# A fused attention and mixture-of-experts block: five shared-expert tiles moved into the start, their gates on GpSimd, and the small transposes behind the weighing

## The reference, cut to what matters

```
def _L0_attn_ref(x, Wq, Wk, Wv, norm_w, Wo, bo, diff_weight):
    ...
    scores = jnp.einsum('bqhif,bkhif->ibhqk', qs, ks_) * scale
    atts = jax.nn.softmax(scores, axis=-1)
    att = atts[0] - diff_weight * atts[1]
    o = jnp.einsum('bhqk,bkhe->bqhe', att, vs)
    rms = jax.lax.rsqrt(jnp.mean(o * o, axis=(-2, -1), keepdims=True) + eps)
    normed = (o * rms * norm_w).reshape(b, s, e)
    return (normed @ Wo.T + bo) * (1.0 - diff_weight)

def _L0_ffn_ref(x, Wg, Ws1, Ws3, Ws2, We1, We3, We2):
    gates = jax.nn.sigmoid(xf @ Wg)
    vals, idx = jax.lax.top_k(gates, TOP_K)
    ...
    shared = jax.nn.silu(xf @ Ws1) * (xf @ Ws3) @ Ws2
    h = jax.nn.silu(jnp.einsum('td,edf->tef', xf, We1)) * jnp.einsum('td,edf->tef', xf, We3)
    routed = jnp.einsum('tef,efd,te->td', h, We2, w)
    out = (shared + routed) / (N_SHARED + TOPK)
    ...
x = x + attention(xn) + ffn(xn)
```

## Time and profile before

| | |
|---|---|
| median of 3 runs | 604.8 us (603.62 to 604.98) |
| profiled execution | 604.48 us, of which the span from first to last instruction is 602.5 us |
| PE busy | 95% of the span |
| DVE busy | 78% |
| ACT busy | 67% |
| POOL busy | 36% |
| mean granted TensorE clock | 0.976 of full speed |

### The profile page before, as it was taken

How to read it: one execution, slowest core, us unless ns; L and a number is a source line. 1 busy time by engine, 2 the same in 40 slices (tenths; PEclk the granted TensorE clock), 3 DMA queues, 4 the chain that set the end, 5 groups by cost and what they waited for, 6 DMA issues and landing times.

```text
span 602.5 us, 13620 instructions
## 1 busy us (share of the span) xinstructions
PE 569.5 (95%) x4725; PEld 337.4 (56%) x4725; DVE 470.8 (78%) x1012; ACT 401.7 (67%) x808; POOL 217.4 (36%) x296
## 2 busy tenths in 40 slices
PE   7797999998999989999999999999999999999994
PEld 6574545554555554466655655566556656665443
DVE  4989778887888887787777787887877878877294
ACT  4363565766676756777677767777677767776682
POOL 5540053555555554033232343222433333232320
PEclk9788898999999999999999999999999999999899
DMA  5995300250116221576346834476444845430292
GB/s 162 211 183 119 103 16 14 70 136 25 37 37 147 58 79 38 148 192 201 101 128 149 247 100 140 128 196 173 141 138 122 219 146 143 123 98 14 77 302 58
DMA packets 62531, 74.07 MB, mean 123 GB/s; under 512 B 7296, under 2 KB 42496, under 8 KB 62464
## 3 DMA queue, kind: packets, MB, share of 16 engines
q1 hardware_dynamic: 57952, 64.00, 40.8%
q0 software_dynamic: 4352, 8.95, 4.6%
q10 hardware_dynamic: 160, 0.26, 0.2%
HBM read 40.08 MB, written 15.80 MB: 93 GB/s over the span
## 4 chain that ended last, share of the span: by engine, by line
PE 68%; DVE 15%; issue 6%; ACT 3%; POOL 2%; DMA 2%; SPq 2%; POOLq 0%; DVEq 0%; ACTq 0%
PE O L1163 17%; PE T L1134 10%; PE F L1203 8%; DVE rowmax L842 7%; PE F L1217 7%; PE T L1139 4%; PE F L1200 3%; PE F L1097 2%; PE F L1182 2%; DVE hid L861 2%; PE O L1124 2%; PE O L1029 1%; SPq L261 1%; DVE base L934 1%; PE F L1087 1%
## 5 line engine op out<-in xcount | busy, mean ns | idle before, releaser
L648 ACT ACTIVATE probs<-T 128x512 f32<-128x512 f32 x372 | 202.4, 596 | 107.9 <-PE T L1139 70.0
L842 DVE TENSOR_REDUCE rowmax<-S 128x1 f32<-128x512 f32 x370 | 237.9, 682 | 30.1 <-PE S L1124 27.7
L1124 PE MATMUL S<-kop,qop 32*128 32x512 f32 x370 | 140.9, 456 | 3.3 <-DVE rowmax L842 2.2
L1163 PE MATMUL O<-probs,vop 128*32 128x512 f32 x1024 | 125.5, 607 | 0.0
L482 POOL DMA_INDIRECT yt<-ysb,xst x72 | 71.0, 986 | 138.3 <-DMA yt<-ysb,xst 125.7
L1134 PE MATMUL T<-qop,kop 32*128 32x512 f32 x372 | 99.7, 500 | 1.4 <-ACT probs L648 1.0
L1139 PE MATMUL T<-mop,ones_r 2*128 2x512 f32 x372 | 78.5, 400 | 0.0
L471 POOL DMA_INDIRECT xs<-xn,slot_i x64 | 62.5, 976 | 42.9 <-DVE rowmax L842 31.0
L648 ACT ACTIVATE probs<-V 128x512 f32<-128x512 f32 x126 | 76.1, 604 | 1.8 <-PE S L1139 0.9
L1203 PEld LDWEIGHTS F<-xsT,wrt_all 128*128 128x128 f32 x576 | 67.0, 191 | 13.2 <-issue 9.4
L842 DVE TENSOR_REDUCE rowmax<-V 128x1 f32<-128x512 f32 x59 | 40.7, 689 | 43.1 <-PE S L1124 32.5
(11 more groups left out here) (168 smaller groups left out, 903.7 us busy)
## 6 DMA issues: line engine op xcount, KB each, us to landing
wrt_all<-in_wexp SPq DMA_DIRECT2D x72, 384.0 KB, 3.9
qop<-qparts SPq DMA_DIRECT2D x64, 128.0 KB
kop<-kparts SPq DMA_DIRECT2D x62, 128.0 KB
xs<-xst SPq DMA_DIRECT2D x12, 387.0 KB, 7.0
xst<-xs SPq DMA_DIRECT2D x36, 129.0 KB, 4.0
base<-in_x SPq DMA_DIRECT2D x8, 256.0 KB, 4.5
xn<-yt SPq DMA_DIRECT2D x8, 256.0 KB, 5.0
out_x<-base SPq DMA_DIRECT2D x7, 256.0 KB, 4.1
```

The lines of the kernel that those rows point to most:

```text
L648: A(probs[:, n % NP, :], banks[e_bank[n]][:, :], ACT.Exp, scale=SCALE).then_inc(s_p, 1)
L842: V.reduce_max(rowmax[hf][:, x_map[n], c, x_row[n]:x_row[n] + 1], banks[x_bank[n]][:, :], AX).then_inc(s_mx, 1)
L1124: mm(banks[x_bank[n]][:, :], qop[b % 2][at:at + BAND, c, t * P:(t + 1) * P], kop[b % 2][at:at + BAND, c, :], start=True, stop=True, tile_p ...
L1163: last = mm(O[VW * j:VW * (j + 1), :], vop[b % 2][:, t, (4 * g + j) // MAPS, :], probs[:, n % NP, :], start=(t == 0), stop=(t == QT - 1), ...
```

## The change

Five shared tiles (`EARLY`), 1,280 tokens, leave the pairs 4 to 19. The first two run in the lead, in bank V: `up` for one side in one slot (-7, -6 and -4, -3), `down` at slots -4 and -1. The third starts at slot -1, the others at pairs 0 and 1, with their `down` in pairs 0, 1 and 2. Their gates are on GpSimd, which can't read PSUM here: ScalarE makes the tanh and copies both halves out (`h1c`, `h3c`), GpSimd does three 128 x 512 operations, ScalarE copies the result out, and GpSimd adds it. The fillers of those places fall away.

The other 22 blocks of 128 tokens run in 18 pairs, 2 to 19: one block ("half tile") in most, two in pairs 6, 10, 14 and 18. The arithmetic done is the same as before.

Third, on PE the small tasks `do_nT`, `do_mT`, `do_q` go from before the weighing to behind it and behind `do_xsT`; ScalarE's copies of them go into the next pair; `do_xsT` uses F1 in place of F0. This holds in all pairs, the routed ones too. The prefix sums of the routing go from pair 2 to the end of pair 1.

```
+    EARLY = 5
+    SH_TILES = 18
+    TWO = (6, 10, 14, 18)
-    SH_AT = [8 + 2 * i for i in range(SH_TILES)]
+    SH_AT = [4 + 2 * i for i in range(SH_TILES)]
+    SH_N = [2 if at // 2 in TWO else 1 for at in SH_AT]
+    E_UP, E_UP1, E_DOWN = {0: -7, 1: -4}, {0: -6, 1: -3}, {0: -4, 1: -1}
+    G_GATE, G_ADD = [-5, -2, 0, 1, 3], [-3, 0, 1, 2, 5]
-    PREFIX_AT = 2
+    PREFIX_AT = 1
...
+            def gate_early(e):
+                h = hid[e % 2][:, :, :].rearrange("p c t -> p (c t)")
+                gp.wait_ge(s_eth, e + 1)
+                gp.wait_ge(s_ehc, e + 1)
+                G.tensor_tensor(h, h, h1c[e % 2][:, :], ALU.mult).then_inc(s_egt, 1)
+                gp.wait_ge(s_egt, 3 * e + 1)
+                G.tensor_tensor(h, h, h1c[e % 2][:, :], ALU.add).then_inc(s_egt, 1)
+                gp.wait_ge(s_egt, 3 * e + 2)
+                gp.wait_ge(s_e3c, e + 1)
+                G.tensor_tensor(h, h, h3c[e % 2][:, :], ALU.mult).then_inc(s_egt, 1)
+
+            def add_early(e):
+                gp.wait_ge(s_eyc, e + 1)
+                gp.wait_ge(s_bias, e // 2 + 1)
+                rows = base[:, 2 * e:2 * e + 2, :].rearrange("p s d -> p (s d)")
+                G.tensor_tensor(rows, rows, yc[:, :], ALU.add).then_inc(s_eys, 1)
...
+            def early_h1(e):
+                bank = F[2 if e in E_UP else 0]
+                act.wait_ge(s_e1, e + 1)
+                if e >= 2:
+                    act.wait_ge(s_ey, e - 1)
+                    act.wait_ge(s_egt, 3 * (e - 2) + 3)
+                A(hid[e % 2][:, :, :].rearrange("p c t -> p (c t)"), bank[:, :], ACT.Tanh, scale=0.5).then_inc(s_eth, 1)
+                A(h1c[e % 2][:, :], bank[:, :], ACT.Copy).then_inc(s_ehc, 1)
+
+            def early_h3(e):
+                act.wait_ge(s_e3, e + 1)
...
+                A(h3c[e % 2][:, :], F[2 if e in E_UP else 1][:, :], ACT.Copy).then_inc(s_e3c, 1)
...
+            def up_early(e, side):
+                bank = F[2 if e in E_UP else side]
+                claim(["V" if e in E_UP else f"F{side}"], (s_ehc, s_e3c)[side], e + 1)
...
+            def down_early(e):
+                bank = F[2 if e in E_UP else 1]
+                claim(["V" if e in E_UP else "F1"], s_eyc, e + 1)
+                pe.wait_ge(s_egt, 3 * e + 3)
...
             def do_xsT(r):
-                bank = F[0]
-                claim(["F0"], s_xtc, r + 1)
+                bank = F[1]
+                claim(["F1"], s_xtc, r + 1)
...
                     do_mT(0)
                 x = norm_at(slot - 2)
                 if x is not None:
                     do_xT(x)
-                if -9 < slot < -2:
+                if slot == -8:
                     keep_busy(LEAD_FILL, ["V"])
-                if slot == -1:
-                    keep_busy(28, ["V"])
...
+                if slot == -1:
+                    up_early(2, 0)
+                    up_early(2, 1)
...
+                if p < EARLY - 2:
+                    down_early(p + 2)
                 j = tile_at(2 * p - 2)
                 if j is not None:
                     down(j)
-                if bare(p):
-                    keep_busy(8 if p < 4 else 4, ["F1"])
+                if bare(p) and p >= 4:
+                    keep_busy(4, ["F1"])
 
                 scores(p, 1)
                 j = tile_at(2 * p)
                 if j is not None:
                     up(j, 0)
                     up(j, 1)
-                if bare(p):
-                    keep_busy(16 if p < 4 else 8, ["F1"])
+                if p < EARLY - 3:
+                    up_early(p + 3, 0)
+                    up_early(p + 3, 1)
...
                 scores(p, 2)
+                if p < PAIRS - 1:
+                    weigh(2 * p)
+                weigh(2 * p + 1)
+                r = routed(tile_at(2 * p + 2))
+                if r is not None:
+                    do_xsT(r)
+                if p == PREFIX_AT:
+                    do_prefix()
                 if w == 1 and b >= 1:
                     do_nT(b - 1)
                 if w == 2:
...
-                if p < PAIRS - 1:
-                    weigh(2 * p)
-                weigh(2 * p + 1)
-                r = routed(tile_at(2 * p + 2))
-                if r is not None:
-                    do_xsT(r)
```

More of the change, by code:

```diff
@@ L85, in shared, with shared_by, width @@
         return SH_AT.index(TILE_AT[j]) if j is not None and TILE_AT[j] in SH_AT else None
+    def shared_by(b):
+        return sum(1 for row in SH_ROW if row < QT * (b + 1))
+    def width(j):
+        i = shared(j)
+        return TOK if i is None else P * SH_N[i]
     def tile_of(r):
@@ L188, in differential_attention_moe_block @@
         ysb = [sb(f"ysb{i}", [P, 2, D]) for i in range(2)]
+        h1c = [sb(f"h1c{i}", [P, FC * TOK]) for i in range(2)]
+        h3c = [sb(f"h3c{i}", [P, FC * TOK]) for i in range(2)]
+        yc = sb("yc", [P, TOK])
         def scratch(at, blocks):
@@ L687, in _ @@
                     normalise(x)
+                for e in E_UP:
+                    if E_DOWN[e] == slot:
+                        early_y(e)
+                for e in E_UP:
+                    if E_UP[e] == slot:
+                        early_h1(e)
+                    if E_UP1[e] == slot:
+                        early_h3(e)
                 if slot in Z_AT:
@@ L925, in combine @@
                 dve.wait_ge(s_rt, R_STEPS)
[L926 removed]
+                added(b)
                 if b < BATCH - 1:
@@ L1165, in weigh @@
                 last.then_inc(s_av, 1)
+            def up_early(e, side):
+                bank = F[2 if e in E_UP else side]
+                claim(["V" if e in E_UP else f"F{side}"], (s_ehc, s_e3c)[side], e + 1)
+                if e == 0 and side == 0:
+                    pe.wait_ge(s_wsh, 16)
+                pe.wait_ge(s_xTc, e // 2 + 1)
+                for c in range(FC):
+                    at = side * FF + c * P
+                    last = mm(bank[:, c * TOK:(c + 1) * TOK], wsh[:, at:at + P], xT[:, e // 2, e % 2 * TOK:e % 2 * TOK + TOK],
+                              start=True, stop=True)
+                last.then_inc((s_e1, s_e3)[side], 1)
+            def down_early(e):
+                bank = F[2 if e in E_UP else 1]
+                claim(["V" if e in E_UP else "F1"], s_eyc, e + 1)
+                pe.wait_ge(s_egt, 3 * e + 3)
+                for i in range(2):
+                    for c in range(FC):
+                        last = mm(bank[:, i * P:(i + 1) * P], hid[e % 2][:, c, i * P:(i + 1) * P],
+                                  wsh[:, 2 * FF + c * P:2 * FF + (c + 1) * P], start=(c == 0), stop=(c == FC - 1))
+                last.then_inc(s_ey, 1)
             def weights(j, i):
@@ L1199, in up @@
                     if routed(j) is None:
-                        last = mm(bank[:, c * TOK:(c + 1) * TOK], wsh[:, at:at + P], tokens(j), start=True, stop=True)
+                        n = width(j)
+                        last = mm(bank[:, c * n:(c + 1) * n], wsh[:, at:at + P], tokens(j), start=True, stop=True)
                     else:
@@ L1214, in down @@
                 pe.wait_ge(s_hid, j + 1)
-                for i in range(2):
+                n = width(j)
+                h = hid[j % 2][:, :, :].rearrange("p c t -> p (c t)")
+                for i in range(n // P):
                     for c in range(FC):
-                        last = mm(bank[:, i * P:(i + 1) * P], hid[j % 2][:, c, i * P:(i + 1) * P],
+                        last = mm(bank[:, i * P:(i + 1) * P], h[:, c * n + i * P:c * n + (i + 1) * P],
                                   weights(j, i)[:, 2 * FF + c * P:2 * FF + (c + 1) * P], start=(c == 0), stop=(c == FC - 1))
@@ L1237, in _ @@
                     score_max(4 * (slot + LEAD) + i)
-                if slot != -9:
-                    keep_busy(LEAD_FILL, ["F0"] if slot < -9 else ["V"])
+                if slot == 0 - LEAD:
+                    keep_busy(LEAD_FILL, ["F0"])
+                elif slot == -8:
+                    keep_busy(LEAD_FILL, ["V"])
+                for e in E_UP:
+                    if E_DOWN[e] == slot:
+                        down_early(e)
                 if slot == -2:
```

90 lines of the change are left out of this document (63 added, 27 removed).

## The result

The changed kernel took 612.4 us (median of 4, 610.09 to 615.27) where the kernel before took 604.59 beside it (median of 4, 603.62 to 604.98). The ratio is 1.0142, 95% interval 1.01 to 1.0184. In the profile after, `row_max` is line 923, the gates 943 and 951, `score_exp` 1223, the weighing 1252, `do_mT` 1176, `do_xsT` 1293, `up` 1310 (shared), `down` 1329, the early `up` and `down` 1264 and 1274, and GpSimd's gate 478, 480 and 483.

A forecast was written before the change was run, and what follows sets the result against it. PE's order was taken to set the time from pair 4 on, with DVE close behind. Terms -14.5 + 10.5 + 3.0 + 5.0 = +4.0 on 604.48 gave 608.5 us; range 597 to 615, the forecast's own 605 to 611.

The forecast's parts named there:

- the start goes badly: Rival, chance 0.15: PE waits for gates, the clock falls, lead and pairs 0 to 3 cost 13 us: 613.5 us.
- the order: Pairs 6, 10, 14, 18: do_mT behind the weighing no longer waits for the gate; 1.3 us gained, at most 2.2.
- the halves: Half tiles in the 12 one-block pairs of 4 to 19: 1.1 us saved a pair, 13.2 in all, between 7.2 and 16.8.
- signs of being wrong: The forecast is wrong if the routed stretch keeps its length, or pair 4 starts under 4 or over 12 us later.
- The F1 wait: Odd routed pairs: token transposes wait for gate_hid to free F1, 0.56 to 0.76 us each, +10.5 us, bounds 0 and 13.
- The first rival: Routed pairs: the wait for F1 costs nothing, 598 us if all of it is gone; chance 0.20.
- Pairs 4 to 19: Half tiles and the new order of small tasks together: -14.5 us, between -7 and -19.
- the halves don't pay: Rival, chance 0.08: DVE becomes the bound of pairs 4 to 19, gain 8 in place of 14.5: 615 us.
- my low end of 7.2: Half tiles in pairs 4 to 19: DVE's own saving, 12 x 0.6 us, as the least gain.
- The lead: Before pair 0: later router scores 1.9, DVE steps held by GpSimd 0.8, slot -1 0.3; +3.0 us, between +1 and +6.
- Pairs 0 to 3: Early tile work in place of fillers and waits for GpSimd's gates: +5.0 us, between +1 and +8.
- The 2 us over the row's median: Lead: by the shared-port rule every two-input DVE step beside a gate waits, costing some 2 us more.

The follow-up runs named there:

- e3: The kernel before with one edit, token transposes on bank F1 in place of F0: 614.89 us, ratio 1.0107.
- e2: The kernel before with small tasks behind the weighing and token transposes on F1, without early or half tiles: 612.29 us, ratio 1.0058.
- e1: The changed kernel with the old order, old bank and old places of ScalarE's copies from pair 20 on: 605.93 us, ratio 0.9954 to the kernel before.
- e5: e4 with 40 fillers ahead of do_mT(0), in PE's idle spell: 605.81 us, ratio 0.9953 to the kernel before.
- e6: e4 with GpSimd's gates of tiles 0 and 1 done for only 32 of 512 columns: 603.62 us, ratio 0.9968 to the kernel before.
- e9: e7 with GpSimd's third step of gate 1 made to wait for DVE's three small steps before do_mT(0): 608.26 us, ratio 0.9946 to the kernel before.
- e10: e9 with 16 fillers ahead of do_mT(0) and twice the fillers in pairs 20, 21, 58 and 59: 603.52 us, ratio 0.9914 to the kernel before.
- e4: The changed kernel with banks swapped, token transposes on F0 and small tasks (but the first do_mT) on F1: 609.94 us, ratio 1.0003 to the kernel before.
- e7: e4 with ScalarE's copy of the prefix sums ahead of the exponentials of its pair: 610.6 us, ratio 1.0006 to the kernel before.
- e12: The kernel before with only the additional fillers in pairs 20, 21, 58 and 59: 607.23 us, ratio 0.9975.
- e11: The kernel before with small tasks behind the weighing, swapped banks, and more fillers in pairs 20, 21, 58 and 59: 604.49 us, ratio 0.9936.

## Why the prediction was right, and where its terms were not

The medians differ by 7.8 us where +4.0 was forecast; the time lies in the range and the direction is the likeliest one. At 612.4 it is 1.4 above the forecast's own 605 to 611 and nearest to the 613.5 of the rival "the start goes badly". That the sum is no further off is in part luck: the order gave 4.9 us more than I took and the halves 5.2 less, while the start cost 4.1 more and two pairs that I had at nothing 2.8 more. One of my own signs of being wrong came true, if only just: pair 4 starts 12.1 us later, and I had named more than 12.

**The F1 wait: +9.8 us against +10.5, shown.** e3 makes it with the bank alone (+8.7, as in e2; after has a fall of the clock in this stretch besides), e1 takes it away. It agrees in detail too: 0.76 us in pair 31 as worked out from the earlier trace rows, 0.64 in pair 27 against 0.57, and in pair 25 0.76 less the 0.21 that stood before `do_nT` in the earlier trace rows, so 0.55 against 0.56. Pair 26 waits 0.89 where it had waited 0.95 before `do_mT`: zero, as said. The double pairs hide this at first (pairs 32 and 33 show 17.17 against 17.21), since `do_nT` of pair 33 has moved across the mark; pairs 32 to 35 together lost 1.06 us of the 1.32 forecast. The first rival, that this wait costs nothing, is refuted.

**Pairs 4 to 19: -14.1 against -14.5, a sum of two wrong terms.** e2 has the new order without the half tiles and so splits it: 139.79, 133.63, 125.66. The order gave 6.2 us, of which 2.0 lie in pairs 4 and 5, where the clock was granted at 0.91 in the kernel before and at 1.00 in e2; the other 4.2, of which 2.3 in pairs 10, 11, 18 and 19, stand against the 1.3 that I took and are more than my ceiling of 2.2. The halves gave 8.0 where 13.2 was forecast. Two things took the rest. A half tile isn't half: chain of waits, pair 8 of after,

```profile
134.37 0.45 PE F L1329 x4
...
135.70 1.09 PE F L1310 x8
```

`up` costs 1.09 and not 0.96, against 1.92 in the earlier trace rows. And DVE has its say. Double pairs 4 and 8, each with two half tiles, first of e2, then of after:

```profile
89.82:106.50 16.68, 16.50 (x114) 8.18 (x118) 15.49 (x34) 11.49 (x22) 5.81 (x8) 1.00 0.04 13
...
122.89:139.11 16.22, 16.22 (x128) 9.56 (x128) 13.77 (x25) 10.94 (x21) 9.87 (x12) 1.00 0.44 115
```

```profile
100.05:116.92 16.87, 15.59 (x114) 7.66 (x118) 15.24 (x37) 11.00 (x23) 6.24 (x9) 1.00 0.04 12
...
132.64:146.89 14.25, 14.21 (x117) 7.94 (x118) 11.90 (x24) 10.51 (x21) 8.64 (x11) 1.00 0.49 127
```

In pairs 8 and 9 two halves save 1.97 us; in pairs 4 and 5 they save nothing (+0.19). There the chain of waits runs through GpSimd's steps of the routing, from 96.2 to 100.6, and then through DVE's maxima and routing steps until the weighing of pair 4 at 106.92. Of the 5.2 us that are missing this place takes 2.4. The other ten halves saved 0.82 each, not 1.1, and in each double pair of theirs, to 0.3 us, as much as DVE's own work shrank: 1.97 with 1.87 in pairs 8 and 9, 0.90 with 0.68 in pairs 10 and 11 (one half). Over all pairs it is 7.97 with 7.79. That is what a bound by DVE would look like, and it is my low end of 7.2; but PE's work shrank too, and no run has cheaper DVE work alone, so it isn't shown. The DVE prices were right: 0.42 for the gate of 256 columns, and 0.28 for the addition that I took at 0.35. The rival "the halves don't pay" (8 us) was thus half true: the halves did give 8, its mechanism stands in the chain of pair 4, and the better order hid it in the sum.

**The lead: +6.1 against +3.0.** The step that failed is "With 0.3 for slot -1", behind "From there the path is stiff: maxima, `do_mT`, ScalarE's copy, the transfer". The router scores came 1.07 late (1.9 forecast), and the held DVE steps cost 1.7 us where I took 0.8 of my 0 to 2.6. Those two make 2.8 us, against the 2.7 that I had for them in sum. The other 3.3 lie behind `do_mT`: from its start to the first exponential scores it is 3.8 us in the kernel before and 7.2 in after, since `down` of tile 1 and `up` of tile 2 took the place of the transfer as the longest leg, at half clock. With the clock up the same work is worth 0.5: in e5, e6, e9 and e10 the way is 4.35 us. So I had priced slot -1 about right and left out what the idle spell does to its clock, which stood in a rival only. That the holding comes from GpSimd's gates is shown by e6 and e9. The clock went with PE's idle spell ahead of `do_mT`: in the four profiles where it is 3.1 us (after, e1, e4, e7) the clock falls at 49.0 to 50.5, in e5, e9 and e10, where it is 0.4 to 1.4, not before 57. e6 shows that it can fall earlier without that spell, at 41. The Trainium skill (SBUF — State Buffer, section "SBUF: two separate sides") says that whichever of the two engines starts first keeps the shared ports for its whole instruction; the ends of 49.37 beside 49.33 and 50.60 beside 50.55 agree. The 2 us over the row's median that I had worked out by it, and weighed lower, are nearer to the measured 1.7 than my 0.8.

**Pairs 0 to 3: +6.0 against +5.0.** Of this 2.1 us are the place of the prefix copy (e7). The sentence "The prefix sums only move by a pair" was wrong: the copy moved behind the exponentials while PE's next use of the bank stayed put. Much of the rest is tile work at half clock (8.0 us at 0.50 above), the mechanism of the rival "the start goes badly"; the start cost 12.1, near its 13. What I gave in that rival's favour was misread: the earlier trace rows has the 1.7 us of idle time and the granted 0.55 in one stretch, not one behind the other. In every version, and in the kernel before, a fall of the clock begins somewhere between 54 and 64 us. What would hold it there stays open.

**Pairs 20 and 21: +2.8, foreseen by nobody.** The weighing took 3.37 us in pair 20 and 3.36 in pair 21, 1.92 in the kernel before:

```profile
231.83 3.37 PE L1252 MATMUL O<-probs,vop 128*32 128x512 f32 x16
```

That is the granted clock, 0.83 over the stretch, and it isn't the change's alone: e3, which differs from the kernel before in a bank, has 17.83 us there and a fall in pairs 10 and 11 (21.30 us at 0.92), while e5 and e6, with no fall in pairs 20 and 21, take 15.95 and 15.94. The 1.2 us that pairs 58 and 59 gained go with the same thing the other way: the clock falls there in the kernel before (at 559.9) and not in after. Such falls cost 1 to 7 us each. With more fillers in the bare pairs (e10 to e12) there was none in those pairs; they came up elsewhere, in pairs 10, 11, 18 and 19 in e10, 18 and 19 in e11, 22 and 23 in e12. Which pair is hit, and why, stays open.

One reading of the rows was off, and nothing rests on it: the routed pairs take 309.74 / 36 = 8.6 us, of which DVE is busy 6.8, not 6.7 of 8.4.

## What to carry to other kernels

A bank that is freed by the last instruction of an engine's turn is a poor place for whatever another engine does first in the next: ask of every bank who frees it and when, before asking whether it is free; one bank here cost 8.7 us in the routed pairs, and the swap won 3.6 there but lost most of it in the shared ones. Half the size may buy no more than the second busiest engine's own saving, pair by pair and not on average. Of a copy that moves, ask who waits for the bank it empties. Small vector steps on the way to a handover should be kept clear of GpSimd's long operations, if need be by making GpSimd wait for them.

## What the runs showed of the hardware that I had not expected

- A DVE instruction with one input, 128 x 32 elements, is held like one with two: 0.90 us beside a GpSimd operation of 1.26, 0.18 when GpSimd starts behind it (e9).
- A matmul chain with half the columns takes 1.09 us and not half of 1.92 (`up`), while half the number of matmuls takes half (`down`, 0.45 against 0.89).
- The clock can fall in one execution and stay in another behind the same work. In e4 pairs 58 and 59 took 22.95 us, in e9 15.69. Busy by stretch, e4 and then e9:

```profile
557.70:561.00 3.30, 2.87 (x25) 2.27 (x25) 2.09 (x4) 2.69 (x6) 0.00 (x0) 1.00 0.00 0
561.00:564.00 3.00, 2.33 (x24) 1.23 (x22) 2.83 (x13) 1.84 (x6) 1.12 (x2) 1.00 0.00 0
564.00:572.00 8.00, 8.00 (x32) 2.84 (x33) 0.68 (x4) 3.18 (x7) 4.34 (x6) 0.53 0.09 27
572.00:580.65 8.65, 8.65 (x48) 3.92 (x46) 3.32 (x12) 3.09 (x7) 0.00 (x0) 0.50 0.76 213
```

```profile
549.67:553.00 3.33, 2.89 (x25) 2.27 (x25) 2.13 (x4) 2.73 (x6) 0.00 (x0) 1.00 0.00 0
553.00:556.00 3.00, 2.37 (x24) 1.26 (x22) 2.83 (x13) 1.85 (x6) 1.16 (x2) 1.00 0.00 0
556.00:565.36 9.36, 9.36 (x78) 4.16 (x81) 1.77 (x8) 6.14 (x13) 4.32 (x6) 1.00 0.09 28
```

PE is busy 5.20 of 6.30 us ahead of the place in the one and 5.26 of 6.33 in the other, with the same instructions. Then e4 goes on at 1.2 GHz for over 16 us, in which PE is never idle, and e9 at 2.4. A single profile can't show what a change does to such a stretch; count executions.
